# Maxima taken in pairs, spread value matmuls and an earlier weigh in a two-layer decoder

## The chip, the cores and the metric

The kernel runs on one core of a Trainium2 chip. The metric is the time of one execution in microseconds (us) on the device, as the median of several runs. TensorE (PE) multiplies matrices and writes PSUM, VectorE (DVE) reduces and combines, ScalarE (ACT) evaluates exponentials and copies, GpSimd (POOL) helps in a few places, and SyncE (SP) issues DMAs. PSUM has eight banks of 512 fp32 columns. The engines run side by side, each in the order of its own program, and wait for each other by semaphores.

## The reference

Two decoder layers over 1024 tokens of width 128, with a context of 6404 rows: layer 0 is a state space block, cross attention to the context and experts; layer 1 is self attention, cross attention and experts, each followed by a residual and a norm. The part that matters most here is the first cross attention, with 16 heads of size 8 and keys and values that all heads share:

```
kvp = c @ w_kv                       # c: the context rows
k, v = kvp[..., :D_HEAD], kvp[..., D_HEAD:]
attn_score = einsum('bhid,bjd->bhij', qh, k) / sqrt(D_HEAD)
attn_prob = softmax(attn_score, axis=-1)
out = einsum('bhij,bjd->bhid', attn_prob, v)
```

The self attention of layer 1 has the same form with keys and values per head and 1024 of them.

## The kernel before

`decoder` runs the stages one after the other: mamba, context_attention, experts0, self_attention, context_attention1, experts1.

**context_attention** treats 1024 queries x 16 heads as NB = 16 blocks of 1024 (a tile of 128 tokens and 8 heads). A block needs its softmax shift, the maximum of each row over all keys, before its exponentials. So the maxima of block b+1 are worked out while block b is attended:

- *Tiles of maxima.* Per block TILES = 104: 8 heads h, each with NR = 13 ranges r of keys, twelve of 512 and the last of 260 columns. Tile u is head u // 13, range u % 13. TensorE writes a tile (`max_tile`, L796) into one of PLACES = 4 banks of `max_ps`, in turn by the item's number in `order`; VectorE reduces it to one column of `partial` (`maximum`, L981) and so releases the bank (`tile_used`). Before it writes, TensorE waits in `free_place` for the item four places earlier. The matmul has its operands in one half of the array's rows, the score matmul of the block before in the other.
- *Turns.* After tiles 51 and 103 VectorE negates the maxima of four heads (`negate`, L992 to L994); TensorE turns them into rows (`turn_shift`, L803, items "A" and "B", which also take a place in the four banks) and ScalarE copies them into the queries (`take_shift`, L821).
- *Attending.* `attend` has EXPS = 102 steps e, two for each of NCH = 51 chunks of 128 keys (the last has 4). At a step TensorE writes a score tile (`score`, L929) into one of three banks, waiting for the exponential three steps before, then the items of that step (`items_at`, mostly one tile of the next block). ScalarE takes the exponential (`exponentiate`, L965) into one of three buffers of chunks. `weigh` (L918) multiplies a chunk's exponentials with its values and adds up in `acc_ps`: two chunks behind step 6k+2, one behind step 6k+5. Chunks 49 and 50 of a block are weighed behind step 0 of the next one, and ScalarE then copies the sums out (`take_acc`, L955) behind the exponential of step 0.

Items are spread over the steps by a fixed rule, so the order of the four banks is fixed when the program is built.

**The first tiles.** The maxima of block 0 are worked out before there is anything to attend, in a stretch of some 85 us. TensorE's work between those tiles is the queries (`make_queries`, L839, and `subtract_high`, L845, the second half of them one product in ten tiles), and from tile 20 on "jobs": the context's values for this layer (51 matmuls of 8 columns, 13, 13, 13, 11 and 1 to a job, L861), then the keys (L865) and values (L870) of layer 1, the jobs in two banks in turn (one of `score_ps` and `acc_ps`), each copied out by ScalarE.

**self_attention** has the same machinery for 16 blocks (one head each): 16 steps, 16 tiles of maxima, 8 chunks, four probability buffers. Tiles are written at L1539, turned at L1548, scores at L1567, exponentials at L1617, weighs at L1578, maxima at L1630, sums copied at L1601. Chunks 6 and 7 are weighed behind step 0 of the next block.

## Time and profile before

| | us |
|---|---|
| median of 3 runs | 2091.1 |
| lowest, highest | 2088.22, 2096.46 |
| the profiled execution | 2089.03 |
| its span, first to last instruction | 2087.3 |

| stretch, us from the start of the span | what runs |
|---|---|
| 182 to 266 | first tiles, queries, jobs |
| 266 to 1230 | context attention, blocks 0 to 14, maxima of the next block beside them |
| 1230 to 1294 | block 15, no maxima beside it |
| 1475 to 1710 | self attention |

Over the whole span TensorE's matmuls are busy for 1963.3 us (94%), VectorE for 1571.0 (75%) and ScalarE for 1360.1 (65%). A matmul's record shows its start and a modelled end, and matmuls overlap, so TensorE's share says little; starts are what to read. The rows of a timeline give the start and the duration, and in brackets how long the engine idled before and which instruction released it. "PEld" is TensorE's load of weights ahead of a matmul. An fp32 matmul of a weigh is shown as two records, so a weigh has 8. PEclk is the granted clock of TensorE, 1.00 for 2.4 GHz and 0.5 for 1.2 GHz.

### The profile page before, as it was taken

To read this page: it belongs to the slowest core of one execution; us is meant where nothing else is said; L and a number is where in the kernel's file an instruction comes from. 1 tells how busy PE (TensorE), PEld (TensorE's weight loads), DVE (VectorE), ACT (ScalarE), POOL (GpSimd) and SP (SyncE) were. 2 spreads that over 40 slices of the span, in tenths; PEclk is the share of its full clock that TensorE was granted. 3 is DMA by queue.
4 is the path that set the end of the run, shared out by engine and by line. 5 is a ranking of instruction groups with operands and counts; after the bars stand their busy time and mean duration, and the time that the engine had idled before them with its cause. 6 is when DMAs were issued, how large, how long until landed. Compare 5 with 4: busy or idle time off the path is not lost. (4 is left out here: it accounts for less than half of the span.)

```text
span 2087.3 us, 38311 instructions
## 1 busy us (share of the span) xinstructions
PE 1963.3 (94%) x15036; PEld 1030.1 (49%) x15036; DVE 1571.0 (75%) x3006; ACT 1360.1 (65%) x2404; POOL 98.9 (5%) x84
## 2 busy tenths in 40 slices
PE   7778999999999999999999999898999988999898
PEld 2225744444444444444444444676344435777755
DVE  7995899999999999999999951333788854444344
ACT  5333488888888888888888887332588863333421
POOL 1660000000000000000000000001000000000000
PEclk8998899999999999999999999898999998999999
DMA  4210000000000000000000000110000000000011
GB/s 144 71 61 0 1 2 2 2 1 2 2 1 2 2 1 2 2 2 1 2 2 1 2 1 1 31 38 18 0 1 1 2 1 1 1 1 0 11 33 28
DMA packets 22853, 24.73 MB, mean 12 GB/s; under 512 B 5712, under 2 KB 20080, under 8 KB 22432
## 3 DMA queue, kind: packets, MB, share of 16 engines
q1 hardware_dynamic: 21504, 20.37, 3.3%
q8 instruction: 111, 1.82, 0.4%
q10 hardware_dynamic: 1184, 2.10, 0.3%
q14 instruction: 54, 0.44, 0.1%
HBM read 21.74 MB, written 0.59 MB: 11 GB/s over the span
## 5 line engine op out<-in xcount | busy, mean ns | idle before, releaser
L981 DVE TENSOR_REDUCE sb_max_partial<-ps_max_ps 128x1 f32<-128x512 f32 (+1 forms) x1664 | 976.3, 662 | 61.1 <-PE ps_max_ps L796 60.4
L965 ACT ACTIVATE sb_probs<-ps_score_ps 128x512 f32<-128x512 f32 (+1 forms) x1632 | 874.0, 597 | 111.0 <-PE ps_score_ps L929 65.6
L929 PE MATMUL ps_score_ps<-sb_q_stack,sb_key_stack 64*128 64x512 f32 x1632 | 586.6, 444 | 3.9 <-ACT sb_probs L965 3.4
L796 PE MATMUL ps_max_ps<-sb_key_stack,sb_q_stack 64*128 64x512 f32 (+1 forms) x1560 | 555.7, 438 | 0.0
L918 PE MATMUL ps_acc_ps<-sb_probs,sb_val_ones 128*32 128x256 f32 x6528 | 465.0, 387 | 0.2 <-ACT sb_probs L965 0.2
L929 PEld LDWEIGHTS ps_score_ps<-sb_q_stack,sb_key_stack 64*128 64x128 f32 x1632 | 276.8, 184 | 326.2 <-ACT sb_probs L965 267.9
L796 PEld LDWEIGHTS ps_max_ps<-sb_key_stack,sb_q_stack 64*128 64x128 f32 x1560 | 265.1, 184 | 9.6 <-DVE sb_max_partial L981 7.3
L918 PEld LDWEIGHTS ps_acc_ps<-sb_probs,sb_val_ones 128*32 128x32 f32 x6528 | 156.4, 108 | 207.0 <-issue 144.2
L1630 DVE TENSOR_REDUCE sb_s_max_partial<-ps_s_ps 128x1 f32<-128x512 f32 x256 | 159.9, 683 | 21.7 <-PE ps_s_ps L1539 21.6
L1617 ACT ACTIVATE sb_s_probs<-ps_s_ps 128x512 f32<-128x512 f32 x256 | 140.7, 597 | 25.6 <-PE ps_s_ps L1567 16.6
L1914 DVE TENSOR_SCALAR_CACHE_REDUCE sb_x_scores<-ps_x_score_ps 128x1024 f32<-128x1024 f32 (+1 forms) x56 | 62.1, 1111 | 82.4 <-PE ps_x_score_ps L1855 82.4
L1894 ACT COPY sb_x_turned<-ps_x_turn_ps 128x512 f32<-128x512 f32 (+1 forms) x52 | 29.6, 569 | 131.9 <-PE ps_x_turn_ps L1870 131.9
L1882 PE MATMUL ps_x_acc_ps<-sb_val,sb_x_turned 128*128 128x128 f32 (+1 forms) x816 | 109.1, 277 | 1.2 <-DVE sb_x_turned L1894 0.9
L1855 PE MATMUL ps_x_score_ps<-sb_key_T,sb_x_q_buf 128*128 128x512 f32 (+1 forms) x208 | 101.3, 590 | 8.7 <-DVE sb_x_q_buf L1923 8.7
L1567 PE MATMUL ps_s_ps<-sb_s_q_stack,sb_s_key_stack 64*128 64x512 f32 x256 | 102.2, 460 | 4.2 <-ACT sb_s_probs L1617 4.2
L1539 PE MATMUL ps_s_ps<-sb_s_key_stack,sb_s_q_stack 64*128 64x512 f32 x256 | 102.5, 458 | 1.5 <-DVE sb_s_q_stack L1493 1.5
L1882 PEld LDWEIGHTS ps_x_acc_ps<-sb_val,sb_x_turned 128*128 128x128 f32 (+1 forms) x816 | 99.5, 192 | 3.5 <-issue 1.0
L1272 DVE SCALAR_TENSOR_TENSOR sb_e_acc<-ps_e_out_ps,sb_e_gates,sb_e_acc 128x128 f32<-128x128 f32 x136 | 36.7, 343 | 79.7 <-PE ps_e_out_ps L1252 79.7
L1261 ACT ACTIVATE sb_e_hidden<-ps_e_hid_ps,sb_e_b 128x1024 f32<-128x1024 f32 x34 | 37.7, 1113 | 78.4 <-PE ps_e_hid_ps L1241 78.4
L444 PE MATMUL ps_mamba_ps<-sb_xpad,sb_ident 128*128 128x512 f32 x128 | 65.2, 632 | 22.7 <-POOL sb_xpad L509 22.7
L613 ACT ACTIVATE sb_val<-sb_delta,sb_a_neg 128x1024 f32<-128x1024 f32 x32 | 36.6, 1148 | 74.2 <-DVE sb_key_T L670 69.6
L1578 PE MATMUL ps_s_ps<-sb_s_probs,sb_s_val_ones 128*32 128x256 f32 x1024 | 79.1, 392 | 0.2 <-ACT sb_s_probs L1617 0.2
(269 smaller groups left out, 1827.7 us busy)
## 6 DMA issues: line engine op xcount, KB each, us to landing
sb_val<-c_rows SPq DMA_DIRECT2D x16, 512.0 KB, 3.7
sb_e_w<-L_ffn_rW SPq DMA_DIRECT2D x30, 128.0 KB, 2.1
sb_e_w<-L_ffn_W_T SPq DMA_DIRECT2D x24, 128.0 KB, 2.1
sb_ctx_T<-ctx_T SPq DMA_DIRECT2D x1, 1664.0 KB, 7.7
sb_ctx_T<-ctx_T ACTq DMA_DIRECT2D x1, 1538.0 KB, 8.7
sb_x_T<-x_T SPq DMA_DIRECT2D x1, 512.0 KB, 3.8
sb_x_tok<-x ACTq DMA_DIRECT2D x1, 512.0 KB, 11.1
sb_e_w<-L_ffn_sW SPq DMA_DIRECT2D x4, 128.0 KB, 2.4
```

What stands on the lines that cost most here:

```text
L796: nc.tensor.matmul(bank((blk, u))[:, 0:n], queries, keys, start=True, stop=True).then_inc(tile_ready, 1)
L918: ins = nc.tensor.matmul(acc_ps[32 * q:32 * q + 32, 0:QUART], k.val_ones[:, v, :], probs[:, v % 3, q * QUART:(q + 1) * QUART], start=(v == ...
L929: nc.tensor.matmul(score_ps[:, e % 3, :], k.key_stack[rows(blk), c * P:(c + 1) * P], q_stack[rows(blk), blk // 2, j * HALF:(j + 1) * HALF] ...
L965: nc.scalar.activation(probs[0:n, c % 3, j * HALF:(j + 1) * HALF], score_ps[0:n, e % 3, :], ACT.Exp).then_inc(exp_done, 1)
L981: nc.vector.tensor_reduce(partial[:, blk % 2, h, r:r + 1], bank((blk, u))[:, 0:RANGES[r][1]], AX.X, ALU.max).then_inc(tile_used, 1)
L1539: nc.tensor.matmul(bank((blk, u)), q_stack[rows(blk), blk // 2, t * P:(t + 1) * P], key_stack[rows(blk), blk // 2, r * HALF:(r + 1) * HALF ...
L1567: nc.tensor.matmul(score_ps[:, n % 3, :], key_stack[rows(blk), blk // 2, c * P:(c + 1) * P], q_stack[rows(blk), blk // 2, j * HALF:(j + 1) ...
L1578: ins = nc.tensor.matmul(acc_ps[32 * q:32 * q + 32, 0:QUART], val[:, v, head(blk), :], probs[:, n % BUFS, q * QUART:(q + 1) * QUART], star ...
L1617: nc.scalar.activation(probs[:, n // 2 % BUFS, (e % 2) * HALF:(e % 2 + 1) * HALF], score_ps[:, n % 3, :], ACT.Exp).then_inc(exp_done, 1)
L1630: nc.vector.tensor_reduce(partial[:, blk % 2, t, r:r + 1], bank((blk, u)), AX.X, ALU.max).then_inc(tile_used, 1)
L1855: ins = nc.tensor.matmul(score_ps[:, local % 2, (g % 2) * HALF:(g % 2) * HALF + n], q_buf[:, s, :], k.key1_T[:, g * HALF:g * HALF + n], st ...
L1882: ins = nc.tensor.matmul(acc_ps[:, s, 0:D], turned[0:keys, local % 2, j * P:(j + 1) * P], k.val1[0:keys, c0 + j, :], start=(c0 + j == 0), ...
```

## The change

Four edits, in the two attention stages.

1. *Pairs.* Where two tiles u and u+1 of one head (neither of them range 12, nor u range 11) stand in places 0, 1 or 2, 3 one behind the other, VectorE waits until both are written and takes both maxima in one instruction over two banks, `[128, 2, 512]` to two columns (`pair_maxima`, L998 of the changed kernel). It adds 2 to `tile_used` at its end. All other tiles are reduced one by one.
2. *Values.* The 51 small value matmuls are no jobs any more: they are issued one at a time behind tiles 21, 22, 24, 25, 27 ... 96, all into one bank of `score_ps` (`value`, L865), and ScalarE copies them out in two instructions at tile 96. TensorE waits for that copy before it attends. The second half of the queries uses one bank instead of two in turn, and the jobs start with the keys.
3. *Context attention's end of a block.* Chunk 49 is weighed behind step 101, ahead of turn B, instead of behind step 0 of the next block; chunk 50 stays behind step 0.
4. *Self attention's end of a block.* Chunk 6 is weighed behind step 15, ahead of turn B; chunk 7 and the copy of the sums go from behind step 0 to behind step 1.

```diff
+            v_ready, v_taken = k.sem("ctx_v_ready"), k.sem("ctx_v_taken")
-            val0_jobs = [(c, min(13, NCH - 1 - c)) for c in range(0, NCH - 1, 13)] + [(NCH - 1, 1)]
...
+            def paired(blk, u):
+                return (u % NR < NR - 2 and place[(blk, u)] % PLACES in (0, 2)
+                        and place[(blk, u + 1)] == place[(blk, u)] + 1)
...
-                return score_ps[:, i % 2, :]
+                return score_ps[:, 0, :]
...
-                    pe.wait_ge(q_done, i - 3 if i < HB else i - 1)
+                    pe.wait_ge(q_done, i - 3 if i < HB else i)
...
+            v_ps = score_ps[:, 1, 0:NCH * HD].rearrange("p (c e) -> p c e", e=HD)
+            def value(pe, c):
+                n = P if c < NCH - 1 else TAIL
+                ins = nc.tensor.matmul(v_ps[0:n, c, :], k.ctx_T[:, c * P:c * P + n], k.w_kv[:, HD:2 * HD], start=True,
+                                       stop=True)
+                if c == NCH - 1:
+                    ins.then_inc(v_ready, 1)
+            def take_values(act):
+                act.wait_ge(v_ready, 1)
+                nc.scalar.copy(k.val_ones[:, 0:NCH - 1, 0:HD], v_ps[:, 0:NCH - 1, :])
+                nc.scalar.copy(k.val_ones[0:TAIL, NCH - 1, 0:HD], v_ps[0:TAIL, NCH - 1, :]).then_inc(v_taken, 1)
...
+            VALUE_AT = {FIRST_JOB + 1 + 3 * c // 2: c for c in range(NCH)}
...
                     if e == 0 and blk > 0:
-                        weigh(pe, blk - 1, NCH - 2)
                         weigh(pe, blk - 1, NCH - 1)
...
+                weigh(pe, blk, NCH - 2)
                 if blk + 1 < NB:
                     issue(pe, (blk + 1, "B"))
...
+            def pair_maxima(dve, blk, u):
+                h, r, at = u // NR, u % NR, place[(blk, u)] % PLACES
+                dve.wait_ge(tile_ready, blk * TILES + u + 2)
+                nc.vector.tensor_reduce(partial[:, blk % 2, h, r:r + 2], max_ps[:, at:at + 2, :],
+                                        AX.X, ALU.max).then_inc(tile_used, 2)
...
-                            maximum(dve, blk, u)
+                            if u > 0 and paired(blk, u - 1):
+                                pair_maxima(dve, blk, u - 1)
+                            elif not paired(blk, u):
+                                maximum(dve, blk, u)
... self_attention
-                    if e == 0 and blk > 0:
-                        weigh(pe, blk - 1, NT - 2)
+                    if e == 1 and blk > 0:
                         weigh(pe, blk - 1, NT - 1)
...
+                weigh(pe, blk, NT - 2)
                 if blk + 1 < NB:
                     issue(pe, (blk + 1, "B"))
...
-                    if e == 0 and blk > 0:
+                    if e == 1 and blk > 0:
                         take_acc(act, blk - 1)
```

The 689 pairs are 44 in block 0 and 43 in each other block, always the same ones. This list has the tiles of the next block in the order in which a block's steps issue them; a line is one cycle of six steps, "w" a weigh, brackets a pair; tiles without brackets are taken alone. The first line has steps 0 to 2. `A` and `B` are the turns.

```
                                   1    (2   3)  ww(only behind later cycles)
 (4   5)  (6   w   7)  (8   9)  ww
(10  11)  12   w  13  (14  15)  ww
(16  17) (18   w  19) (20  21)  ww
(22  23)  24   w  25  (26  27)  ww
(28  29) (30   w  31) (32  33)  ww
(34 35) (36  37)   w   38  39 (40  ww
 41) (42  43)  w (44  45) (46   ww
 47) (48  49)  w  50   51 (52   ww
 53) (54  55)  w (56  57) (58   ww
 59) A 60 (61  w  62)  63  64   ww
(65  66) (67   w  68) (69  70) (71   ww
 72) (73  74)  w (75  76)  77   ww
 78  (79  80)  w (81  82) (83   ww
 84) (85  86)  w (87  88)  89   ww
 90  (91  92)  w (93  94) (95   ww
 96) (97  98)  w (99 100) (101  ww
102) 103  next block's 0   w  B
```

VectorE, the first half of block 1's maxima, before and then changed. The first 52 maxima stand in one run there, L992 to L994 negate them:

```order
L981 TENSOR_REDUCE sb_max_partial<-ps_max_ps 128x1 x52
L992 TENSOR_REDUCE sb_neg_max<-sb_max_partial 128x4
L993 CAST sb_neg_part<-sb_neg_max 128x4
L994 TENSOR_TENSOR sb_neg_part<-sb_neg_max,sb_neg_part 128x4
```
```order
L991 TENSOR_REDUCE sb_max_partial<-ps_max_ps 128x1 x2
L998 TENSOR_REDUCE sb_max_partial<-ps_max_ps 128x2 x5
L991 TENSOR_REDUCE sb_max_partial<-ps_max_ps 128x1 x2
L998 TENSOR_REDUCE sb_max_partial<-ps_max_ps 128x2 x5
L991 TENSOR_REDUCE sb_max_partial<-ps_max_ps 128x1 x2
L998 TENSOR_REDUCE sb_max_partial<-ps_max_ps 128x2 x6
L991 TENSOR_REDUCE sb_max_partial<-ps_max_ps 128x1 x2
L998 TENSOR_REDUCE sb_max_partial<-ps_max_ps 128x2 x5
L991 TENSOR_REDUCE sb_max_partial<-ps_max_ps 128x1 x2
L1009 TENSOR_REDUCE sb_neg_max<-sb_max_partial 128x4
L1010 CAST sb_neg_part<-sb_neg_max 128x4
L1011 TENSOR_TENSOR sb_neg_part<-sb_neg_max,sb_neg_part 128x4
```

52 instructions became 30, of which 22 are pairs (here 128x2 is the output, one column for each of the two tiles).

TensorE in the stretch of the first tiles, from tile 18 on (L796 and L801 are tiles, L861 and L865 values, L839 and L844 queries, L879 a job of layer 1's keys), before and then changed:

```order
L796 MATMUL ps_max_ps<-sb_key_stack,sb_q_first 128x512
L839 MATMUL ps_score_ps<-sb_x_T,sb_wq_rep 128x512
L796 MATMUL ps_max_ps<-sb_key_stack,sb_q_first 128x512 x2
L861 MATMUL ps_score_ps<-sb_w_kv,sb_ctx_T 128x8 x13
L796 MATMUL ps_max_ps<-sb_key_stack,sb_q_first 128x512
L845 MATMUL ps_score_ps<-sb_q_stack,sb_minus_low 128x512
L796 MATMUL ps_max_ps<-sb_key_stack,sb_q_first 128x512
L796 MATMUL ps_max_ps<-sb_key_stack,sb_q_first 128x260
L861 MATMUL ps_acc_ps<-sb_w_kv,sb_ctx_T 128x8 x13
L796 MATMUL ps_max_ps<-sb_key_stack,sb_q_first 128x512 x3
L861 MATMUL ps_score_ps<-sb_w_kv,sb_ctx_T 128x8 x13
```
```order
L801 MATMUL ps_max_ps<-sb_key_stack,sb_q_first 128x512
L865 MATMUL ps_score_ps<-sb_w_kv,sb_ctx_T 128x8
L801 MATMUL ps_max_ps<-sb_key_stack,sb_q_first 128x512
L865 MATMUL ps_score_ps<-sb_w_kv,sb_ctx_T 128x8
L801 MATMUL ps_max_ps<-sb_key_stack,sb_q_first 128x512
L850 MATMUL ps_score_ps<-sb_q_stack,sb_minus_low 128x512
L879 MATMUL ps_score_ps<-sb_ctx_T,sb_wk 128x512
L801 MATMUL ps_max_ps<-sb_key_stack,sb_q_first 128x512
L865 MATMUL ps_score_ps<-sb_w_kv,sb_ctx_T 128x8
L801 MATMUL ps_max_ps<-sb_key_stack,sb_q_first 128x260
L865 MATMUL ps_score_ps<-sb_w_kv,sb_ctx_T 128x8
L801 MATMUL ps_max_ps<-sb_key_stack,sb_q_first 128x512 x2
```

The bursts of 13 small matmuls are gone; one stands behind most tiles, and the keys' jobs come earlier.

TensorE at the end of block 0 (L929 and L939 are scores, L918 and L928 weighs, L803 and L808 turn B), before and then changed:

```order
L796 MATMUL ps_max_ps<-sb_key_stack,sb_q_stack 128x260
L929 MATMUL ps_score_ps<-sb_q_stack,sb_key_stack 128x512 x2
L796 MATMUL ps_max_ps<-sb_key_stack,sb_q_stack 128x512
L918 MATMUL ps_acc_ps<-sb_probs,sb_val_ones 32x256 x4
L803 MATMUL ps_max_ps<-sb_ident,sb_neg_part 2x128 x4
L929 MATMUL ps_score_ps<-sb_q_stack,sb_key_stack 128x512
L796 MATMUL ps_max_ps<-sb_key_stack,sb_q_stack 128x512
L918 MATMUL ps_acc_ps<-sb_probs,sb_val_ones 32x256 x8
```
```order
L801 MATMUL ps_max_ps<-sb_key_stack,sb_q_stack 128x260
L939 MATMUL ps_score_ps<-sb_q_stack,sb_key_stack 128x512 x2
L801 MATMUL ps_max_ps<-sb_key_stack,sb_q_stack 128x512
L928 MATMUL ps_acc_ps<-sb_probs,sb_val_ones 32x256 x8
L808 MATMUL ps_max_ps<-sb_ident,sb_neg_part 2x128 x4
L939 MATMUL ps_score_ps<-sb_q_stack,sb_key_stack 128x512
L801 MATMUL ps_max_ps<-sb_key_stack,sb_q_stack 128x512
L928 MATMUL ps_acc_ps<-sb_probs,sb_val_ones 32x256 x4
```

Four of the eight matmuls behind the next block's step 0 moved ahead of the turn.

## Rows read from the trace of the kernel before

**Rows 1.** Line 955 (copy of the sums): range of durations, first and last start, us.

```profile
L955 ACT COPY sb_gathered<-ps_acc_ps x2: 373/373/373, 653.3 to 717.6; 128x256 f32<-128x256 f32 x2
```

**Rows 2.** VectorE's groups by shape: count, busy us, mean ns, idle before and releaser.

```profile
L981 DVE TENSOR_REDUCE sb_max_partial<-ps_max_ps 128x1 f32<-128x512 f32 x1536 | 939.6, 682 | 61.1 <-PE ps_max_ps L796 60.4
...
L1914 DVE TENSOR_SCALAR_CACHE_REDUCE sb_x_scores<-ps_x_score_ps 128x1024 f32<-128x1024 f32 x48 | 58.8, 1225 | 80.3 <-PE ps_x_score_ps L1855 80.3
L981 DVE TENSOR_REDUCE sb_max_partial<-ps_max_ps 128x1 f32<-128x260 f32 x128 | 53.6, 419 | 0.0
```

**Rows 3.** Waits, whole run: who waited for whom, us in total, times, longest.

```profile
PEld ps_score_ps L929 <- ACT sb_probs L965: 267.9, 711, 0.7
...
DVE sb_max_partial L981 <- PE ps_max_ps L796: 60.4, 86, 7.5
```

**Rows 4.** Timeline of TensorE, one cycle: start us, us, engine, line, operation, tiles.

```profile
709.56 0.49 PE L796 MATMUL ps_max_ps<-sb_key_stack,sb_q_stack 64*128 64x512 f32 x1
...
709.89 0.39 PE L796 MATMUL ps_max_ps<-sb_key_stack,sb_q_stack 64*128 64x512 f32 x1
...
711.02 0.50 PE L796 MATMUL ps_max_ps<-sb_key_stack,sb_q_stack 64*128 64x512 f32 x1
...
711.36 0.39 PE L796 MATMUL ps_max_ps<-sb_key_stack,sb_q_stack 64*128 64x512 f32 x1
711.72 0.49 PE L929 MATMUL ps_score_ps<-sb_q_stack,sb_key_stack 64*128 64x512 f32 x1
711.72 0.50 PE L796 MATMUL ps_max_ps<-sb_key_stack,sb_q_stack 64*128 64x512 f32 x1
...
713.15 0.50 PE L796 MATMUL ps_max_ps<-sb_key_stack,sb_q_stack 64*128 64x512 f32 x1
```

**Rows 5.** Timeline of ScalarE in the last block, two groups of exponentials.

```profile
1251.70 2.61 ACT L965 ACTIVATE sb_probs<-ps_score_ps 128x512 f32<-128x512 f32 x5 [0.23 <-PE ps_score_ps L929]
...
1255.29 2.61 ACT L965 ACTIVATE sb_probs<-ps_score_ps 128x512 f32<-128x512 f32 x5 [0.23 <-PE ps_score_ps L929]
```

**Rows 6.** Timeline of VectorE, eight tiles, the last one of 260 columns.

```profile
710.12 4.62 DVE L981 TENSOR_REDUCE sb_max_partial<-ps_max_ps 128x1 f32<-128x512 f32 x8 [0.17 <-PE ps_max_ps L796]
```

**Rows 7.** Timeline of all engines: maxima, and a tile's weight load behind the second.

```profile
684.17 2.47 DVE L981 TENSOR_REDUCE sb_max_partial<-ps_max_ps 128x1 f32<-128x512 f32 x4
...
685.50 0.18 PEld L796 LDWEIGHTS ps_max_ps<-sb_key_stack,sb_q_stack 64*128 64x128 f32 x1
```

**Rows 8.** Timeline of TensorE, cycle with turn A: tiles 59 and 61.

```profile
686.93 0.49 PE L929 MATMUL ps_score_ps<-sb_q_stack,sb_key_stack 64*128 64x512 f32 x1
...
688.23 0.39 PE L929 MATMUL ps_score_ps<-sb_q_stack,sb_key_stack 64*128 64x512 f32 x1
```

**Rows 9.** Timeline of all engines at a block's end.

```profile
714.27 0.64 PE L918 MATMUL ps_acc_ps<-sb_probs,sb_val_ones 128*32 128x256 f32 x8
...
715.54 0.60 PE L803 MATMUL ps_max_ps<-sb_ident,sb_neg_part 128*2 128x128 f32 x4 [0.63 <-DVE sb_neg_part L994]
...
716.49 1.07 PE L918 MATMUL ps_acc_ps<-sb_probs,sb_val_ones 128*32 128x256 f32 x16
...
717.50 0.49 PE L929 MATMUL ps_score_ps<-sb_q_stack,sb_key_stack 64*128 64x512 f32 x1
...
718.02 0.60 ACT L965 ACTIVATE sb_probs<-ps_score_ps 128x512 f32<-128x512 f32 x1
```

**Rows 10.** Stretches: length, busy us of PE PEld DVE ACT POOL, PEclk, DMA share, GB/s.

```profile
197.00:220.00 23.00, 23.00 (x101) 20.19 (x101) 7.66 (x13) 2.85 (x8) 0.00 (x0) 0.56 0.00 0
220.00:266.00 46.00, 46.00 (x223) 32.39 (x221) 42.24 (x76) 22.37 (x40) 0.00 (x0) 1.00 0.00 1
...
460.00:1230.00 770.00, 759.98 (x7445) 347.66 (x7441) 741.22 (x1318) 672.83 (x1259) 0.00 (x0) 1.00 0.01 1
...
1475.00:1700.00 225.00, 219.28 (x1658) 88.62 (x1660) 190.69 (x376) 174.38 (x318) 0.00 (x0) 0.99 0.01 1
```

**Rows 11.** Timeline at a block's start in self attention: ScalarE's second exponential.

```profile
1609.14 0.60 ACT L1617 ACTIVATE sb_s_probs<-ps_s_ps 128x512 f32<-128x512 f32 x1
```

More of the change, by code:

```diff
@@ L880, in copy_job @@
                 act.wait_ge(job_ready, i + 1)
[L881 to L887 removed]
+                if i < KEYS:
+                    c0, cols = key_jobs[i]
                     ins = nc.scalar.copy(k.key1_T[:, c0:c0 + cols], src[:, 0:cols])
                 else:
[L890 removed]
+                    c, m = val_jobs[i - KEYS]
                     n = P if c < NCH - 1 else TAIL
@@ L1013, in _ @@
                             subtract_high(pe, MINUS_AT[u])
+                        if u in VALUE_AT:
+                            value(pe, VALUE_AT[u])
                         for i in jobs_at(u):
@@ L1025, in _ @@
                     pe.wait_ge(job_copied, EARLY_JOBS)
+                    pe.wait_ge(v_taken, 1)
                     for blk in range(NB):
                         attend(pe, blk)
-                    for v in range(NCH - 2, NCH):
-                        weigh(pe, NB - 1, v)
+                    weigh(pe, NB - 1, NCH - 1)
                 @block.scalar
@@ L1715, in _ @@
                         attend(pe, blk)
-                    for v in range(NT - 2, NT):
-                        weigh(pe, NB - 1, v)
+                    weigh(pe, NB - 1, NT - 1)
                 @block.scalar
```

26 lines of the change are left out of this document (7 added, 19 removed).

## Prediction

> **What bounds the kernel now.** I read the page first, then the table of waits, then the timelines of one block of context attention, because 15 of its 16 blocks are alike and last 64.3 us each [rows 1]: 15 of those are 965 of the 2089 us. By busy shares VectorE looks like the limit there (1536 reductions of 512 columns, 0.682 us each, most of them there [rows 2]). The waits say otherwise: VectorE waited 60.4 us for TensorE over all 16 blocks, while TensorE's score matmuls waited 267.9 us for ScalarE's exponentials [rows 3]. The timelines show a loop of six half chunks. I call it a cycle. Its six scores s0 to s5 (e = 6k+3 to 6k+8) each have a tile behind them, t0 to t5; one weigh stands behind t2 and two behind t5. From the starts of the tiles t0, t1, t3, t4, t5 and the next t0 [rows 4]: 0, 0.33, 1.46, 1.80, 2.16, 3.59 us. The loop: s0, three exponentials, s5 (which may start once the exponential of s2 is done, 2.16), double weigh, next s0, 1.43 later. The last block has no maxima at all and ScalarE's groups still start 3.59 apart (1251.70 to 1255.29) [rows 5]. So a faster VectorE cannot shorten a cycle; a tile that keeps TensorE waiting ahead of s5, or ahead of the double weigh, lengthens it.
>
> **The pairs: cost of an instruction.** A reduction of 512 columns takes 0.682 us, one of 260 0.419, so 252 columns cost 0.263, 1.04 ns each, and 512 more cost 0.53; the widest VectorE reading of two banks, 1024 columns, takes 1.225, 0.54 over the 512 [rows 2]. A pair is then 1.22 us long. Singles follow each other at 0.60 (seven steps, one of them of the short tile, before the last 0.42 of 4.62 us [rows 6]: 4.20 in seven), so a pair holds VectorE 0.60 + 0.53 = 1.13 against 1.20 for two singles. Bounds: 1.20 (nothing saved) and 1.10. With 43 pairs a block it saves VectorE 43 x 0.07 = 3 us of a block, off the path. The Trainium skill, "VectorE: DVE Perf Modes", in the section on the TRN2 errata, says that a fixed latency is paid once per instruction and advises large tiles; that speaks for the pairs, but it prices VectorE alone, and the sum does not change by it.
>
> **The pairs: cost of the places.** Four banks hold tiles, and tile u may be issued when tile u-4 is released. Both banks of a pair are released when the pair ends, 1.22 us plus TensorE's reaction after it starts. The reaction: a reduction that ended at 685.45 (684.17 + 0.60 + 0.68) let a weight load start at 685.50, 0.05 later [rows 7]. So release is 1.27 after the start, and a pair cannot start before its second tile is ready, 0.56 after that tile's issue (709.56 to 710.12 [rows 4, 6]), or about 0.46 for a matmul of 0.39 instead of 0.49.
>
> Which tiles are pairs is in the list of one block. The pattern where a pair spans the double weigh (t5 | t0), (t1 t2), (t3 t4), "split", goes so: pair (t5 t0) starts at 0.56, when t0 is ready; (t1 t2) follows 1.13 later at 1.69 and releases t1's bank at 2.96. The next t5 stands in that bank, so it is issued at 2.96 instead of 2.16, the double weigh waits behind it, and the next s0 comes at 2.96 + 1.43 = 4.39. That is 0.80 us more than 3.59, and nothing gives it back: t0 must be issued again before the chain restarts. On the way t3 waits too (1.83 for 1.46), which is covered by the longer wait.
>
> In the aligned pattern, (t0 t1) (t2 t3) (t4 t5), the pair (t0 t1) starts at 0.33 + 0.46 = 0.79 and releases at 2.06; t4 waits from 1.80 to 2.06, s5 goes 0.23 behind it at 2.29, next s0 at 3.72: 0.13 more.
>
> The cycles of one block in the order of the list, each walked the same way:
> - Tiles 4 to 9 and the block's start: 0, the banks are still free.
> - 10 to 15, 16 to 21, 22 to 27, 28 to 33: aligned, 4 x 0.13 = 0.5.
> - 34 to 40 (seven tiles; 40 needs pair 36, 37, released at about 3.1, where now it goes at about 2.5, an estimate from 2.16 and 0.3 for the seventh tile): 0.6.
> - 41 to 46, 47 to 52, 53 to 58: split, 3 x 0.80 = 2.4.
> - 59 to 64 with turn A (61 needs pair 58, 59, released at 1.83, now issued at 688.23 - 686.93 = 1.30 [rows 8], less what s5 would wait anyway): 0.4.
> - 65 to 71 (seven; 71 needs pair 67, 68, which starts at 2.0): 0.8.
> - 72 to 77: split, 0.8. 78 to 83 (78 is single, so pair 79, 80 starts at 1.16): 0.3. 84 to 89: split, 0.8. 90 to 95: 0.1. 96 to 101: split, 0.8.
>
> Sum of the cycles: 0.5 + 0.6 + 2.4 + 0.4 + 0.8 + 0.8 + 0.3 + 0.8 + 0.1 + 0.8 = 7.5 us a block.
>
> **The end of a block.** Pair (101, 102) now stands ahead of tile 103 on VectorE, though 102 was read the moment it was ready. So 103, the negated maxima and turn B are 0.53 later. The weigh of chunk 49 moves ahead of turn B. A weigh costs 0.43 (1.07 for 16 against 0.64 for 8 [rows 9]); it starts behind the weigh of 714.27, at about 714.7, and is over at 715.1, before the turn of 715.54 (now 0.5 later). It is hidden there, and s1 of the next block, now at 717.50 behind two weighs, loses 0.43 of wait and gains 0.53: 0.1 later. ScalarE's exponential behind the copy of the sums (718.02) moves by the same 0.1. What covers the weigh is TensorE's wait for VectorE; if 103 came early the weigh would cost its 0.43 there and save it behind. Net 0.1 a block. Per block 7.6, for 15 blocks 114 us.
>
> **The values.** Before, 51 small value matmuls stand in four bursts and a last one; the granted clock of 197 to 220 is 0.56 (mostly 1.2 GHz) with TensorE busy for all 23.00 us, and 1.00 (2.4 GHz) in the 46 us behind [rows 10]. The change spreads them one by one between tiles, with a job of full width in nearly every third gap, as in the stretch behind that holds its clock. If the clock stays up, the 20 us or so at the lower level shrink by half: 10 us. I take off 4: at full clock tiles come every 0.7 us on average but 0.23 to 0.45 apart between two jobs, and there pairs make TensorE wait for a bank (b+3 needs b's pair: 0.46 + 1.27 = 1.73 against three gaps, short by about 0.6 where no job falls into them, some 7 times). Net -6; bounds -10 and +3 (clock falls anyway). The copies (two instead of five) lie beside other work; the second half of the queries has one bank in turn instead of two, but ten tiles (over 5 us) apart: 0.
>
> **Self attention.** Weigh 6 goes ahead of turn B, which here waits for nobody, so turn B and e = 0 move by +0.43; weigh 7 goes behind e = 1, so that score comes about 0.5 earlier and the exponential of e = 2, behind the copy of the sums, gains some 0.1: now the exponential of e = 1 waits at 1609.14 for that copy [rows 11]. VectorE's third tile starts when it did. I take -0.1 x 15 = -1; bounds -4 and +3 (0.2 each way a block).
>
> **Sum.** 2089 + 114 - 6 - 1 = 2196 us for the profiled execution. The median of the runs before is 2091.1, 2 us higher; forecast 2198.
>
> **Rivals.**
> 1. *VectorE is the bound after all.* The Trainium skill, "Perfetto Trace Analysis", section "Identifying Performance Opportunities", has the most-contended engine by occupancy be optimised first. In this kernel the mechanism would be: a VectorE that runs 3 us a block less lets each block end 3 us earlier, 15 x 3 = 45, and with the clock's 6: 2040. For it: in block ends it does hold turn B. Against: the last block's cycle [rows 5]. 0.03.
> 2. *The places do not bind* (the other side): if TensorE's order had slack where I see none, for example releases seen early enough, only block ends (0.43 saved x 15 = 6), the clock (10) and self attention (1) are left: 2091 - 17 = 2074. It decides for this case if t5 of a split cycle is issued before 2.3 us after t0. For it: TensorE waits for ScalarE 268 us, which looks like slack. Against: the 2.96 lies beyond the 2.16 whatever ScalarE does. 0.05.
> 3. *Half of the chain is absorbed*, e.g. since split cycles do not keep their phase: 4 us a block, 60 - 7: 2144. 0.05.
> 4. *The clock falls in context attention*, since TensorE idles 0.8 in 4.4 us. Against: self attention works more sparsely (1658 matmuls in 225 us, 7.4 per us, against 7445 in 770 us, 9.7, times 3.59/4.39 = 7.9) at a clock of 0.99 [rows 10]. The Trainium skill, "TensorE: Matmul & The Clock Gate", section "A second HAM failure mode: psum-queue depth-cycling", tells of a kernel whose clock swung in just such short waits for PSUM banks; no run here shows it. The price, from the part of a cycle that is TensorE's (1.43 + 0.56, doubled): +2 us x 17 x 15 = 500 at worst; 2400 if it falls half of the time. 0.03.
>
> **How the numbers follow.** The forecast, places that bind, has the remaining 0.84: 2198. Its own range: 1.10 or 1.20 a pair changes a split cycle by -0.06 or +0.14 (two banks deep) and an aligned one by as much, some 0.5 to 1.3 us a block, 8 to 20 in all, and the walks of the odd cycles are worth as much again; with -10 to +3 for the values and -4 to +3 for self attention: 2152 to 2235. Rival 3 lies just under; I leave it and the rest out (0.16). A change under 0.5% (10 us) cannot be told from none here: faster 0.07 (rivals 1 and 2, less 0.01 for a result between), same 0.02, slower 0.91.
>
> **What would show it.** The profile after should have: blocks of about 72 us between copies of the sums; pairs of 1.22 us, 689 of them; VectorE's wait for TensorE up from 60 to some 200 us (a block of 72 less 43 x 1.13 for pairs, 18 x 0.35 to 0.60 for singles and 1 to 2 for the negated maxima, 15 times); a wait of the tiles' weight loads for the maxima of over 50 us, now none of the long ones; split cycles of 4.4 beside aligned ones of 3.7; the granted clock at 1.0 from 197 to 220. Wrong if blocks stay at 64 us or below, if a pair is much under 1.1 us, or if the clock row shows fives from 270 on.

## The result and the profile after

The changed kernel takes **2231.9 us** (median of 4 runs, 2228.67 to 2234.29), the kernel before 2092.36 beside it: 1.0666 times the time, 95% interval 1.064 to 1.0692. It is 140 us slower; forecast were 2198 us (+107) and 2152 to 2235. The profiled execution is one of 2231.78 us, with a span of 2230.1. All kernels below compute the whole reference. Some executions (of the kernel before, most of the kernel before with pairs, one of free_pairs) are nearly 40 us longer than the others at a lower mean granted clock (0.95 for 0.97); no ratio below rests on them, and the section on the last block is about them.

Line 965 of the changed kernel is the copy of the sums that was line 955 in [rows 1]:

```profile
L965 ACT COPY sb_gathered<-ps_acc_ps x2: 367/368/368, 632.6 to 706.4; 128x256 f32<-128x256 f32 x2
```

A block lasts 73.8 us and lasted 64.3 [rows 1]. The difference times 15 is 142 us, about the whole loss of 140; what the other stages gain and lose nearly cancels. The groups of VectorE by shape (as [rows 2]) and TensorE's weight loads of scores and of tiles:

```profile
L998 DVE TENSOR_REDUCE sb_max_partial<-ps_max_ps 128x2 f32<-128x1024 f32 x689 | 815.4, 1220 | 194.3 <-PE ps_max_ps L801 190.4
...
L939 PEld LDWEIGHTS ps_score_ps<-sb_q_stack,sb_key_stack 64*128 64x128 f32 x1632 | 272.9, 184 | 269.0 <-ACT sb_probs L975 165.5 <-issue 81.9 <-ACT sb_q_stack L826 6.2
L801 PEld LDWEIGHTS ps_max_ps<-sb_key_stack,sb_q_stack 64*128 64x128 f32 x1560 | 252.8, 184 | 168.6 <-DVE sb_max_partial L998 163.1
```

TensorE's tiles wait 163.1 us for pairs, where they had waited 7.3 for maxima; for exponentials its scores wait 165.5 instead of 267.9 [rows 3]; and VectorE waits 190.4 for TensorE instead of 60.4. Each waits for the other, as in a loop whose buffers come back too late. A "split" cycle, first TensorE, then VectorE (a row "x2" is two matmuls in a row, here t0 and t1):

```profile
661.99 0.72 PE L801 MATMUL ps_max_ps<-sb_key_stack,sb_q_stack 64*128 64x512 f32 x2
...
665.04 0.50 PE L801 MATMUL ps_max_ps<-sb_key_stack,sb_q_stack 64*128 64x512 f32 x1 [0.39 <-DVE sb_max_partial L998]
665.47 1.07 PE L928 MATMUL ps_acc_ps<-sb_probs,sb_val_ones 128*32 128x256 f32 x16
...
666.47 0.49 PE L939 MATMUL ps_score_ps<-sb_q_stack,sb_key_stack 64*128 64x512 f32 x1
```
```profile
662.63 2.36 DVE L998 TENSOR_REDUCE sb_max_partial<-ps_max_ps 128x2 f32<-128x1024 f32 x2 [0.99 <-PE ps_max_ps L801]
```

Pair (t5 t0) starts at 662.63, 0.64 us behind t0; the second pair ends at 662.63 + 2.36 = 664.99, t5 is issued at 665.04, the double weigh behind it, and the next s0 at 666.47: a cycle of 4.48, where before it was 3.59.

### The profile page after: what moved, and what is told of

It reads as the page before. It is cut to its first block and busy times, and to the rows that moved or that the text cites. A ratio compares the mean times of both kernels' runs of the same rounds, so it can differ in the third digit from the quotient of the medians.

```text
span 2230.1 us, 38309 instructions
## 1 busy us (share of the span) xinstructions
PE 2045.1 (92%) x15036; PEld 1064.0 (48%) x15036; DVE 1550.3 (70%) x2317; ACT 1358.0 (61%) x2401; POOL 99.0 (4%) x84
## 5 line engine op out<-in xcount | busy, mean ns | idle before, releaser
L998 DVE TENSOR_REDUCE sb_max_partial<-ps_max_ps 128x2 f32<-128x1024 f32 x689 | 815.4, 1220 | 194.3 <-PE ps_max_ps L801 190.4
L801 PE MATMUL ps_max_ps<-sb_key_stack,sb_q_stack 64*128 64x512 f32 (+1 forms) x1560 | 573.0, 441 | 57.3 <-DVE sb_max_partial L998 56.7
L939 PE MATMUL ps_score_ps<-sb_q_stack,sb_key_stack 64*128 64x512 f32 x1632 | 580.3, 443 | 3.9 <-ACT sb_probs L975 3.4
L928 PE MATMUL ps_acc_ps<-sb_probs,sb_val_ones 128*32 128x256 f32 x6528 | 465.1, 387 | 0.2 <-ACT sb_probs L975 0.2
L939 PEld LDWEIGHTS ps_score_ps<-sb_q_stack,sb_key_stack 64*128 64x128 f32 x1632 | 272.9, 184 | 269.0 <-ACT sb_probs L975 165.5
L801 PEld LDWEIGHTS ps_max_ps<-sb_key_stack,sb_q_stack 64*128 64x128 f32 x1560 | 252.8, 184 | 168.6 <-DVE sb_max_partial L998 163.1
L928 PEld LDWEIGHTS ps_acc_ps<-sb_probs,sb_val_ones 128*32 128x32 f32 x6528 | 156.5, 109 | 206.7 <-issue 112.6
L991 DVE TENSOR_REDUCE sb_max_partial<-ps_max_ps 128x1 f32<-128x512 f32 (+1 forms) x286 | 156.2, 565 | 24.8 <-PE ps_max_ps L801 24.0
```

What stands on the lines that cost most here:

```text
L801: nc.tensor.matmul(bank((blk, u))[:, 0:n], queries, keys, start=True, stop=True).then_inc(tile_ready, 1)
L928: ins = nc.tensor.matmul(acc_ps[32 * q:32 * q + 32, 0:QUART], k.val_ones[:, v, :], probs[:, v % 3, q * QUART:(q + 1) * QUART], start=(v == ...
L939: nc.tensor.matmul(score_ps[:, e % 3, :], k.key_stack[rows(blk), c * P:(c + 1) * P], q_stack[rows(blk), blk // 2, j * HALF:(j + 1) * HALF] ...
L991: nc.vector.tensor_reduce(partial[:, blk % 2, h, r:r + 1], bank((blk, u))[:, 0:RANGES[r][1]], AX.X, ALU.max).then_inc(tile_used, 1)
L998: nc.vector.tensor_reduce(partial[:, blk % 2, h, r:r + 2], max_ps[:, at:at + 2, :], AX.X, ALU.max).then_inc(tile_used, 2)
```

## The experiments

### The pairs against everything else

no_pairs is the changed kernel without its pairs, pairs_only the kernel before with them:

```diff
             def paired(blk, u):
-                return (u % NR < NR - 2 and place[(blk, u)] % PLACES in (0, 2)
-                        and place[(blk, u + 1)] == place[(blk, u)] + 1)
+                return False
```

> The changed kernel with no pair anywhere; values, weighs and self attention as changed. Theory P (places: a pair starts only when its second tile is written and gives both banks back only at its end, and TensorE, in order, waits for the bank ahead of the double weigh): blocks of context attention back to 64.0 us (64.3 before, 0.3 less for the weigh ahead of turn B), the first tiles' stretch 6 us shorter than before, self attention 0.1 a block longer as in the changed kernel: 2082 us, 2076 to 2088. Rival M (the moved weighs or values cost the time, or disturb the cycles): blocks stay above 70 us, over 2180.

> The kernel before with the pairs alone. P: blocks of 73.8 us as in the changed kernel (give or take 0.3), 15 x 9.4 = 141 more than before, and 0 to 4 more in the first tiles: 2235 us, 2225 to 2245. M: blocks of 64 to 68, under 2150.

**no_pairs: 2080.44 us**, ratio 0.9946 (0.9929 to 0.9963). Blocks:

```profile
L964 ACT COPY sb_gathered<-ps_acc_ps x2: 367/367/367, 644.3 to 708.2; 128x256 f32<-128x256 f32 x2
```

63.9 us. So the pairs cost 151 us: 15 x (73.8 - 63.9) = 148 in the blocks and 4.5 in the first tiles (79.3 us from the first maximum to the first exponential with pairs, 74.8 without); the other edits gain. **pairs_only: 2289.12 us** in the median, above the range expected, and 2249.26 in the profiled execution, above it too; its blocks are 74.2 to 74.6 and the loss is there as well. The other three executions (2287 to 2295) are those of the section on the last block.

The other edits one by one: values_only is the kernel before with the spread values, weigh_only the kernel before with chunk 49 ahead of turn B, and no_pairs_self_as_before has both, no pairs and self attention as before.

> The kernel before with the value matmuls spread, and nothing else. The clock stays at 1.0 from about 182 us on, the stretch of the first tiles falls from 85 to 75 us, blocks stay at 64.3: 2081 us (2078 to 2085), the 10 us of the prediction without the 4 that pairs take back.

> The kernel before with the weigh of chunk 49 ahead of turn B, and nothing else. Blocks of 63.9 us instead of 64.3 (0.43 less behind step 0), first tiles as before: 2091 - 15 x 0.44 = 2084.5 us (2082 to 2088).

> The changed kernel without pairs and with self attention as before: values and context attention's weigh alone. Self attention back from 12.63 to 12.53 us a block, and the 2 us by which the stages behind it end earlier in the kernels with the old order: 2091 - 10 - 6.6 = 2075 us (2072 to 2080), 4 us or so under the kernel without pairs (2080.4), the fastest of all.

| kernel | us | ratio, 95% | first tiles | block |
|---|---|---|---|---|
| values_only | 2082.27 | 0.9947 (0.9932 to 0.9962) | 74.9 | 64.3 |
| weigh_only | 2082.82 | 0.9961 (0.9946 to 0.9975) | 83.5 | 63.9 |
| no_pairs_self_as_before | 2075.05 | 0.9915 (0.99 to 0.9931) | 74.9 | 63.9 |

Each gains where it should, and the two together are the fastest kernel of the study. The first tiles of weigh_only, which it leaves alone, took 83.5 us where the kernel before took 85.0, so 1.5 us of such a stretch is no effect of an edit. The clock in the stretch of the values, no_pairs_self_as_before in the first block and weigh_only, which keeps the bursts, in the second (columns as in [rows 10]):

```profile
197.00:220.00 23.00, 22.32 (x100) 15.20 (x99) 20.17 (x34) 8.81 (x15) 0.48 (x2) 1.00 0.00 1
```
```profile
197.00:220.00 23.00, 23.00 (x104) 19.22 (x105) 9.44 (x16) 3.25 (x9) 0.00 (x0) 0.63 0.00 1
```

### What of a pair costs: one instruction, the wait, or the release

A pair does three things. It reads two banks in one instruction, it starts when the second tile is written, and it gives both banks back at its end. Each part alone, in the changed kernel:

```diff
two_for_pair: waits for both, two instructions, both banks released by the second
-                nc.vector.tensor_reduce(partial[:, blk % 2, h, r:r + 2], max_ps[:, at:at + 2, :],
+                nc.vector.tensor_reduce(partial[:, blk % 2, h, r:r + 1], max_ps[:, at, :], AX.X, ALU.max)
+                nc.vector.tensor_reduce(partial[:, blk % 2, h, r + 1:r + 2], max_ps[:, at + 1, :],
                                         AX.X, ALU.max).then_inc(tile_used, 2)
wait_both: the same, but each instruction ends in .then_inc(tile_used, 1)
release_late: singles that start at once; the first of a pair releases nothing, the second two
```

> The changed kernel, but each pair is taken by two single reductions, the first behind the wait for both tiles; both banks are given back by the second. Nothing but the instruction's form differs. P (waiting for both tiles and giving both banks back at the end is what costs): a split cycle = 0.56 to the first reduction, 1.20 to the next pair, 1.33 to the end of its second reduction and TensorE's reaction, 1.43 = 4.52 us (changed kernel 4.47); blocks of about 74.5 us, 2243 us (2230 to 2255). Rival W (the reduction over two banks is itself what hurts, by its form): blocks fall under 70, under 2180.

> As two_for_pair, but each reduction gives back its own bank: only the late start is left. P: split cycle 0.56 + 1.20 + 0.73 + 1.43 = 3.92 us (t1 stands first in its pair, so its bank comes back 0.60 earlier), aligned cycles 3.6; blocks of 66.5 us (64.3 before, 0.3 less for the weigh, six split cycles x 0.33 and some 0.5 for the odd ones), 2125 us (2105 to 2150). If the late start were the whole cost: 2230 or more; if none of it: 2085.

> The changed kernel with single reductions that start as soon as their own tile is there, but both banks of a would-be pair are given back only behind the second: only the late return is left. P: in a split cycle t1's reduction starts at 1.16, t2's at 1.76 and ends at 2.44, so t5 is issued at 2.49: 3.92 us, too; aligned 3.6 to 3.7; blocks of 66.5 to 67, 2130 us (2110 to 2155). Together with wait_both: neither half alone gives the 9.4 us a block, since each moves t5 from 2.16 to about 2.5 and only both to 3.05.

| kernel | us | ratio, 95% | block | split cycle |
|---|---|---|---|---|
| the change | 2231.9 | 1.0666 (1.064 to 1.0692) | 73.8 | 4.48 |
| two_for_pair | 2241.1 | 1.0714 (1.0683 to 1.0745) | 74.35 | 4.53 |
| wait_both | 2128.67 | 1.0174 (1.0144 to 1.0203) | 67.2 | 3.94 |
| release_late | 2142.07 | 1.0236 (1.0206 to 1.0266) | 68.0 | 4.00 |
| no_pairs | 2080.44 | 0.9946 (0.9929 to 0.9963) | 63.9 | 3.59 |

**The form of the instruction is worth 9 us in the good direction** and explains none of the loss. Starting late alone costs 3.3 us a block, releasing late alone 4.1, and both together 10.4. That is more than their sum: the two delays add up in front of the same bank, and each alone is first hidden by a slack that both together can use only once. In a split cycle of no_pairs the reduction of t1 ends 1.86 behind t0 and t5, which takes its bank, goes at 2.17, so some 0.26 us is free. Each half delays the bank by about 0.6 and moves t5 to 2.50 (wait_both) or 2.58 (release_late); both move it to 3.10 (two_for_pair). The same cycle in wait_both, TensorE's t5 and three of VectorE's four singles:

```profile
625.77 0.50 PE L801 MATMUL ps_max_ps<-sb_key_stack,sb_q_stack 64*128 64x512 f32 x1
626.20 1.07 PE L928 MATMUL ps_acc_ps<-sb_probs,sb_val_ones 128*32 128x256 f32 x16
```
```profile
623.83 0.69 DVE L998 TENSOR_REDUCE sb_max_partial<-ps_max_ps 128x1 f32<-128x512 f32 x1 [0.26 <-PE ps_max_ps L801]
624.44 0.68 DVE L1000 TENSOR_REDUCE sb_max_partial<-ps_max_ps 128x1 f32<-128x512 f32 x1
625.03 0.68 DVE L998 TENSOR_REDUCE sb_max_partial<-ps_max_ps 128x1 f32<-128x512 f32 x1
```

The third single, that of t1, ends at 625.71 and t5 goes at 625.77, 2.50 behind t0 (623.27) instead of 3.05. The rest of the cycle is unchanged, 1.43 from t5 to the next s0.

release_late does not have the late return alone: the reductions that give back two banks also start later than others. VectorE at tiles 59 and 60 behind TensorE's:

```profile
636.56 0.49 PE L801 MATMUL ps_max_ps<-sb_key_stack,sb_q_stack 64*128 64x512 f32 x1
...
637.51 0.49 PE L801 MATMUL ps_max_ps<-sb_key_stack,sb_q_stack 64*128 64x512 f32 x1
```
```profile
637.19 0.69 DVE L991 TENSOR_REDUCE sb_max_partial<-ps_max_ps 128x1 f32<-128x512 f32 x1 [0.33 <-PE ps_max_ps L801]
638.08 1.29 DVE L991 TENSOR_REDUCE sb_max_partial<-ps_max_ps 128x1 f32<-128x512 f32 x2 [0.19 <-PE ps_max_ps L801]
```

Tile 59, whose reduction adds 2 to `tile_used`, waits 0.63 us for its start, tile 60, whose reduction adds 1, only 0.57. Both read one bank. The traces show what goes with it: each of the 689 instructions that wait and add 2 has its wait in an instruction of its own ahead of it, here and in the changed kernel; a reduction that adds 1 carries its wait itself (the changed kernel has no such instruction at L990). The wait of a pair in the changed kernel:

```profile
L997 DVEq EVENT_SEMAPHORE  x689: 21/21/21, 183.7 to 1367.0; - x173
```

### Which pairs cost

late_pairs keeps the pairs at t2 t3, t3 t4 or t4 t5 of one cycle (19 of 43, and all of block 0), which I took to be free. Two of them the prediction's own walk should have kept out: (67 68), to which it gave 0.8 us at tile 71, and (2 3), whose cycle it had not walked. free_pairs keeps 11, after what late_pairs showed: t2 t3 or t3 t4, not below tile 12, not (67 68), none in block 0.

```diff
late_pairs
...
+            def late(blk, u):
+                a, b = at_step.get((blk, u), -1), at_step.get((blk, u + 1), -1)
+                return blk == 0 or (a >= 0 and b >= 0 and (a - 3) % 6 in (2, 3, 4) and (b - 3) // 6 == (a - 3) // 6)
+
             def paired(blk, u):
-                return (u % NR < NR - 2 and place[(blk, u)] % PLACES in (0, 2)
+                return (late(blk, u) and u % NR < NR - 2 and place[(blk, u)] % PLACES in (0, 2)
free_pairs
+                return blk > 0 and 12 <= u != 67 and (a - 3) % 6 in (2, 3) and (b - 3) // 6 == (a - 3) // 6
```

> The changed kernel, but from block 1 on only the 19 pairs a block that lie within one cycle at (t2 t3), (t3 t4) or (t4 t5). P: their banks are wanted again only after the double weigh, at 3.59 or later, and are given back by then, so they are free: blocks of 64.0 us, within 0.4 of the kernel without pairs, 2083 us (2077 to 2090). Rival L (each pair costs its share by its length, wherever it stands): 19/43 of 9.4 = 4.2 us a block, blocks of 68.2, 2145 us.

> The changed kernel with only 11 pairs a block from block 1 on, (18 19) (30 31) (44 45) (56 57) (61 62) (69 70) (75 76) (81 82) (87 88) (93 94) (99 100), each at (t2 t3) or (t3 t4) of its cycle, and none in block 0. P: by the walk each bank comes back before it is wanted, so every cycle is as without pairs: blocks of 63.9 us (to 64.2), first tiles 75 us, 2081 us (2077 to 2086), with VectorE's instructions 165 fewer. L (a share for each pair): 11/43 of 9.9 = 2.5 us a block, 2118 us.

**late_pairs: 2116.92 us**, 1.0121 (1.0105 to 1.0137), blocks of 66.1: a plain miss (2077 to 2090 were expected), and not the rival's 2145 either. Twelve of the seventeen cycles are as without pairs; the loss is in tiles 4 to 9 (4.47 for 4.00), 65 to 71 (4.80 for 3.93; tile 71 waits for the pair (67 68)) and the cycles behind (6 7)(8 9), (18 19)(20 21) and (30 31)(32 33): they are longer by 0.24 to 0.34 each. VectorE behind (6 7)(8 9), and TensorE's tile 12 there:

```profile
600.52 2.36 DVE L1008 TENSOR_REDUCE sb_max_partial<-ps_max_ps 128x2 f32<-128x1024 f32 x2 [0.48 <-PE ps_max_ps L811]
```
```profile
602.93 0.39 PE L811 MATMUL ps_max_ps<-sb_key_stack,sb_q_stack 64*128 64x260 f32 x1 [0.18 <-DVE sb_max_partial L1008]
```

Pair (8 9) ends at 602.88 and tile 12 goes at 602.93, where it would go right behind s2 (602.36): two pairs in a row, at t2 t3 and t4 t5, are free for that cycle and not for the next. The pairs (14 15) and (26 27), alone at t4 t5, cost the next cycle nothing (3.59). **free_pairs: 2082.66 us**, 0.9951 (0.9935 to 0.9966), blocks of 64.2: eleven pairs cost 0.3 us a block, and gain nothing. The 0.3 is nearly all in one cycle, tiles 34 to 40 (4.20 for 3.93), behind (30 31): VectorE is late there, and tile 37 waits for the bank of tile 33.

### Is it the tile or the double weigh behind it

weigh_first, the changed kernel with the double weigh ahead of t5, so that s0 does not stand behind both:

```diff
+                    of = e // 6 * 3
+                    if e % 6 == 2 and of > 0:
+                        weigh(pe, blk, of - 2)
+                        weigh(pe, blk, of - 1)
                     for item in items:
                         if item[1] != "B":
                             issue(pe, item)
...
-                    of = e // 6 * 3
...
-                    elif e % 6 == 2 and of > 0:
-                        weigh(pe, blk, of - 2)
-                        weigh(pe, blk, of - 1)
```

> The changed kernel with all pairs, but at steps 6k+2 the double weigh stands ahead of the tile t5 instead of behind it. P: t5's wait for its bank runs beside the weighs; a split cycle falls from 4.47 to about 3.9 us, an aligned one from 3.80 to 3.7, blocks of about 68.5 us: 2152 us (2130 to 2180). If the cost is not the bank wait ahead of the double weigh (M or L): blocks stay at 73 to 74, 2225 to 2235.

**2217.02 us**, 1.0598 (1.0582 to 1.0614). Expected were 2152 (2130 to 2180), the second plain miss, and the other side of that expectation (2225 and more) fails as well. The split cycles fell to 3.78 as expected (3.9), but the aligned ones rose from 3.80 to 4.77. One of those, TensorE and VectorE:

```profile
642.32 0.50 PE L801 MATMUL ps_max_ps<-sb_key_stack,sb_q_stack 64*128 64x512 f32 x1
...
642.66 0.40 PE L801 MATMUL ps_max_ps<-sb_key_stack,sb_q_stack 64*128 64x512 f32 x1
...
642.89 0.39 PE L801 MATMUL ps_max_ps<-sb_key_stack,sb_q_stack 64*128 64x512 f32 x1
644.20 0.49 PE L801 MATMUL ps_max_ps<-sb_key_stack,sb_q_stack 64*128 64x512 f32 x1 [0.92 <-DVE sb_max_partial L998]
```
```profile
642.92 2.35 DVE L998 TENSOR_REDUCE sb_max_partial<-ps_max_ps 128x2 f32<-128x1024 f32 x2 [0.63 <-PE ps_max_ps L801]
```

With the weigh ahead, t5 of the cycle before stands here at the front (642.32, then t0 at 642.66 and t1 at 642.89). The pair (t4 t5) cannot start before t5 is written, at 642.92, so t2, which needs t4's bank, waits until 644.20, 1.31 behind t1. The loop went from s0 to the tiles themselves. The order of tile and weigh mostly chooses which kind of cycle pays for the late release; the whole is 15 us shorter than the change.

### The last block and the clock

> The kernel with the pairs alone once more, whose runs lay at 2249 and three times at 2287 to 2295 where the profile shows 74.2 us a block. P has 2249 and knows no 2290. Rival 4 of the prediction (the granted clock falls in some executions where TensorE waits for banks): then a profile in that state shows fives of the clock in context attention or in the first tiles, for about 80 us in all, since half speed costs half of a stretch. If all runs lie near 2250 the other three remain unexplained.

**2285.96 us** (2283.15 to 2287.39), where the same kernel had had one execution of 2249.26. The blocks are again 74.2; the difference is in the last block. First a stretch mostly of block 14, then the last block and what follows:

```profile
1300.00:1366.00 66.00, 61.13 (x552) 27.96 (x550) 53.92 (x61) 49.95 (x95) 0.00 (x0) 1.00 0.01 1
...
1383.90:1430.00 46.10, 46.10 (x231) 19.05 (x231) 0.00 (x0) 25.20 (x48) 0.00 (x0) 0.50 0.00 1
1430.00:1493.00 63.00, 62.26 (x318) 27.73 (x317) 2.96 (x20) 31.14 (x58) 0.00 (x0) 0.50 0.00 1
```
```profile
1382.86 0.60 PE L808 MATMUL ps_max_ps<-sb_ident,sb_neg_part 128*2 128x128 f32 x4 [1.45 <-DVE sb_neg_part L1006]
```

In the blocks with pairs and their waits the granted clock is 1.00 (2.4 GHz). It falls to 0.50 (1.2 GHz) at 1383.9, just behind the last turn B, for 109 us; block 15, which has no maxima beside it, then takes 101 us from its first to its last exponential where it takes 61 in the other profile of this kernel. Those 40 us are the difference (the two profiled executions are only 34 apart, since this one was 6 us ahead at its first maximum, in stages that no edit touches). Half the clock does not cost half the time here: 109 us at 0.50 cost 40 (a cycle of block 15 takes 6.03 for 3.59). Rival 4's stretch, the blocks with waits, is not where it falls. Ahead of the fall TensorE had waited 1.45 for VectorE. In the other profile of this kernel the same wait was 1.42 and the clock stayed:

```profile
1391.08 0.60 PE L808 MATMUL ps_max_ps<-sb_ident,sb_neg_part 128*2 128x128 f32 x4 [1.42 <-DVE sb_neg_part L1006]
```

So that wait does not decide it. The pairs don't either: the kernel before, beside these runs, had five executions of eight at 2126 to 2131 and three at 2090 to 2093, and later two of thirteen at 2129. There is no trace of those, but their mean granted clock is on record, 0.948 to 0.951 for 0.967 to 0.972, as here 0.952 for 0.971, so they are most likely the same fall. In all, seven of eight executions of the kernel with the pairs alone have it, seven of 32 of the kernel before, and none of four of the change, which has the same pairs. Of the kernels with one of the other edits only one execution of free_pairs (2120.17, clock 0.953) was of this kind. Why it falls in some executions stays open.

## Why the prediction was right, and where it was short

**What bounds a cycle: right.** "a faster VectorE cannot shorten a cycle; a tile that keeps TensorE waiting ahead of s5, or ahead of the double weigh, lengthens it" is what two_for_pair, wait_both and release_late showed one by one. Rival 1 (VectorE is the bound) falls with two_for_pair: the saved VectorE time of 43 pairs is worth 9 us, not 45, and only where the places bind. The Trainium skill's rule in "Perfetto Trace Analysis", section "Identifying Performance Opportunities", to optimise the engine with the highest occupancy first (TensorE it judges by other measures), would have named VectorE, busy for 741 of 770 us [rows 10]; in these blocks it did not hold. Rivals 2 (2074) and 3 (2144) fall with the blocks of 73.8.

**The block's sum: short by a fifth.** Forecast +7.6 us a block, measured +9.4, and 15 x 1.8 = 27 of the missing 34 us are there. The time lies only 3 us under the top of the range. Of the rest, self attention has 2 (below), and 5 lie in stages that no edit touches: between the two profiled executions 1.7 us ahead of the first maximum (183.8 for 182.1), 0.9 between the attentions and 2.2 behind the last copy of self attention (383.4 for 381.2). The first of these is as large between kernels that don't differ there (185.8 in no_pairs, 188.5 in pairs_only), so I do not put it on the change. By the prediction's own terms, each the difference of a cycle between the two traces (block 5; s0 to s0):

| term | forecast | measured |
|---|---|---|
| tiles 4 to 9 | 0 | 0.47 |
| 10 to 33, four aligned | 0.5 | 0.34 + 0.20 + 0.23 + 0.22 = 1.0 |
| 34 to 40 | 0.6 | 0.75 |
| 41 to 58, three split | 2.4 | 0.88 + 0.89 + 0.75 = 2.5 |
| 59 to 64 | 0.4 | 0.48 |
| 65 to 71 | 0.8 | 1.02 |
| 72 to 77, split | 0.8 | 0.77 |
| 78 to 83 | 0.3 | 0.28 |
| 84 to 89, split | 0.8 | 0.88 |
| 90 to 95 | 0.1 | 0.21 |
| 96 to 101, split | 0.8 | 0.87 |
| border | 0.1 | 0.17 |
| sum | 7.6 | 9.4 |

- *"Tiles 4 to 9 and the block's start: 0, the banks are still free" was wrong.* Tile 6 needs the bank of tile 2, four places earlier, and (2 3) is a pair. In this first cycle no double weigh stands behind (2 3), so s0 comes 0.57 behind tile 2 (632.42) and the pair is not over when tile 6 wants the bank. VectorE, then TensorE:

```profile
633.29 2.35 DVE L998 TENSOR_REDUCE sb_max_partial<-ps_max_ps 128x2 f32<-128x1024 f32 x2 [0.60 <-PE ps_max_ps L801]
```
```profile
632.42 0.50 PE L801 MATMUL ps_max_ps<-sb_key_stack,sb_q_stack 64*128 64x512 f32 x1
...
634.57 0.50 PE L801 MATMUL ps_max_ps<-sb_key_stack,sb_q_stack 64*128 64x512 f32 x1
```

  The same cycle before, tiles 4 and 6:

```profile
589.37 0.39 PE L796 MATMUL ps_max_ps<-sb_key_stack,sb_q_stack 64*128 64x512 f32 x1
...
590.47 0.50 PE L796 MATMUL ps_max_ps<-sb_key_stack,sb_q_stack 64*128 64x512 f32 x1
```

  The pair starts 0.30 into the cycle (s0 at 632.99) and ends at 634.51; tile 6 goes at 634.57, 1.58 into the cycle, and before it went at 1.10. That is the 0.47. The next cycle starts with VectorE behind and loses 0.34 instead of 0.13. Together 0.7 of the missing 1.8. The prediction had put this term at nothing without walking it.

- *The start of a pair was mis-sized.* I gave it 0.56 us from the issue of its second tile, the figure of a single [rows 4, 6]; it is 0.64 (662.63 against 661.99). In an aligned cycle I gave 0.46, and it is 0.53:

```profile
649.36 0.40 PE L801 MATMUL ps_max_ps<-sb_key_stack,sb_q_stack 64*128 64x512 f32 x1
...
651.16 0.50 PE L801 MATMUL ps_max_ps<-sb_key_stack,sb_q_stack 64*128 64x512 f32 x1
...
651.50 0.39 PE L801 MATMUL ps_max_ps<-sb_key_stack,sb_q_stack 64*128 64x512 f32 x1
...
652.83 0.49 PE L939 MATMUL ps_score_ps<-sb_q_stack,sb_key_stack 64*128 64x512 f32 x1
```
```profile
649.89 3.58 DVE L998 TENSOR_REDUCE sb_max_partial<-ps_max_ps 128x2 f32<-128x1024 f32 x3 [0.47 <-PE ps_max_ps L801]
```

  Tile t1 at 649.36, the pair at 649.89, t4 at 651.16 (the pair's end, 651.11, and 0.05), and t5 0.34 behind it, not 0.23. A cycle of 3.82 where I had 3.72. The 0.07 to 0.08 is not the wait for two tiles, since wait_both's first single starts 0.56 behind its second tile (623.83 against 623.27). It is not the two banks either, since release_late's singles that add 2 have it as well (0.63, above). It goes with the addition of 2, which has the wait in an instruction of its own; no run has a reduction over two banks without it.
- *The length of a pair was right*: 1.220 us, and the next one follows at 662.63 + 1.14 (2.36 - 1.22), forecast 1.22 and 1.13. The section on the TRN2 errata of the Trainium skill ("VectorE: DVE Perf Modes"), which the prediction names beside it, is about operands in SBUF, and these reductions read PSUM; the sum did not use it.
- *The split cycle* was forecast at 4.39 and is 4.48; the 0.09 is the later start. From t5 on, 1.43 to the next s0, unchanged.

**The values: right.** -6 forecast; the first tiles' stretch went from 84.95 to 79.31 us, -5.6, give or take the 1.5 above. By values_only the spread gains 10.1 (84.95 to 74.87), and by no_pairs against the change the pairs take 4.5 back, where I had 10 and 4. It is the wait for banks that I had named: in that stretch the tiles' weight loads wait 9.4 us for pairs in the change and 4.5 for maxima in no_pairs. The clock of the stretch of [rows 10], in the change:

```profile
197.00:220.00 23.00, 22.12 (x98) 14.95 (x97) 18.36 (x22) 8.20 (x14) 0.00 (x0) 1.00 0.00 0
```

**The end of a block: right in kind.** Chunk 49's weigh is hidden ahead of turn B. In the change that gains 0.43 behind step 0 and the late pair (101 102) takes it back (0.6); without pairs it is 0.43 a block net (64.3 to 63.9), 6.6 us in all by weigh_only's context attention (1025.2 to 1018.6). I had that only in rival 2.

**Self attention: wrong sign, small.** Forecast -0.1 a block, measured +0.1 (12.5 to 12.6). The edit took the exponentials' wait away and made a new one, TensorE's first weigh of a block for the copy of the sums:

```profile
L1625 ACT COPY sb_s_gathered<-ps_s_ps x16: 372/373/373, 1660.6 to 1846.7; 128x256 f32<-128x256 f32 x16
its engine sat idle before it (us, times) until:
  PE ps_s_ps L1602: 0.8, 1
who waited for it (us, times):
  PEld ps_s_ps L1602: 5.5, 15
```

5.5 us in 15 waits. I had followed the copy to ScalarE's next exponential and not to the bank that it frees. no_pairs and no_pairs_self_as_before, which differ by this edit alone, are 5.4 us apart in the median (2080.44, 2075.05), but they were run on two chips, and the intervals of their ratios touch (0.9929 to 0.9963, 0.99 to 0.9931). Their profiled executions are 0.7 apart (2079.35, 2078.61) and show 0.9 between the first and the last copy. Another 2.7 lie behind self attention (383.3 against 380.6 us from the last copy to the end), but values_only, whose self attention is as before, has 383.2 there too, so I cannot put that on the edit.

**The clock: half right.** I gave rival 4 a chance of 0.03, in the blocks with waits. It was 1.00 there in every profile; the rule of the Trainium skill ("TensorE: Matmul & The Clock Gate", section "A second HAM failure mode: psum-queue depth-cycling"), a clock that swings in short waits for banks, did not show with a wait of 0.39 us in a cycle of 4.48. It fell in the last block instead, in some executions.

A slip in the text ahead of the prediction: the first half of block 1's maxima is 31 instructions with 21 pairs, as the list there shows, not 30 with 22. It moved no term, since the cycles were walked one by one.
